# Attention: a third buffer of probabilities, and the copies of the raw output behind other exponentials

## The reference

```
x = x + attention(layernorm(x))   # 2 sequences of 512 tokens, 512 wide, 32 heads of 16
x = x + experts(layernorm(x))     # 8 experts of inner width 800, the best 2 of each token

q, k, v = proj(w_q), proj(w_k), proj(w_v)
scores = einsum('bhqd,bhkd->bhqk', q, k) / sqrt(16)
attn = softmax(scores, axis=-1)
out = einsum('bhqk,bhkd->bhqd', attn, v)
out = out.transpose(0, 2, 1, 3).reshape(B, S, HIDDEN)
return einsum('bse,oe->bso', out, w_o)
```

## Time and profile before

| what | value |
|---|---|
| median of 3 runs | 544.23 us (543.7 to 544.29) |
| the profiled execution, its own time | 544.15 us |
| its span in the trace | 542.4 us |
| PE, DVE, ACT busy over the span | 98%, 71%, 59% |
| the ordinary and whole steps of attention | from about 88 to 253 us |

### The profile page before, as it was taken

One profiled execution on the slowest core, in us unless ns is written; L12 is line 12 of the kernel. 1 busy time (PEld: TensorE's weight loads), 2 busy tenths in 40 slices (PEclk: granted clock), 3 DMA queues, 4 the chain that ended last, 5 costly groups with the idle time before them and its releaser, 6 DMA issues.

```text
span 542.4 us, 10567 instructions
## 1 busy us (share of the span) xinstructions
PE 529.6 (98%) x3925; PEld 390.7 (72%) x3925; DVE 385.8 (71%) x722; ACT 321.1 (59%) x476; POOL 117.3 (22%) x146
## 2 busy tenths in 40 slices
PE   8999999999999999999999999999999999999992
PEld 6887665344433334334878989999999999999991
DVE  7924767999998999943879986836648284666650
ACT  5322115888888878876372465746576575757540
POOL 4400111000120120722001320432342321242112
PEclk9999999999999999999989999999999999999998
DMA  8490367765775470022734797775846747586122
GB/s 304 142 112 6 48 107 91 99 89 90 95 98 72 89 143 14 24 91 100 280 119 171 234 379 250 204 255 111 320 72 219 224 155 267 129 296 159 39 36 38
DMA packets 29743, 78.24 MB, mean 144 GB/s; under 512 B 8572, under 2 KB 9596, under 8 KB 25210
## 3 DMA queue, kind: packets, MB, share of 16 engines
q1 hardware_dynamic: 24394, 68.84, 47.3%
q0 software_dynamic: 5296, 8.69, 8.7%
HBM read 53.11 MB, written 9.32 MB: 115 GB/s over the span
## 4 chain that ended last, share of the span: by engine, by line
PE 93%; DVE 2%; DMA 1%; issue 1%; POOL 1%; ACT 1%; POOLq 0%; DVEq 0%
PE ps L720 17%; PE ps L722 16%; PE ps L721 16%; PE ps_o L735 13%; PE ps L748 7%; PE ps L760 6%; PE ps_m L748 4%; PE ps L788 2%; PE ps_o L720 1%; PE ps_m L1017 1%; PE ps L1069 1%; PE ps L1072 1%; PE ps_o L721 1%; PE ps_o L722 1%; PE ps_m L720 1%
## 5 line engine op out<-in xcount | busy, mean ns | idle before, releaser
L1242 ACT ACTIVATE probs_t<-ps 128x1024 f32<-128x1024 f32 x128 | 125.5, 1023 | 27.6 <-PE ps_o L735 23.3
L1459 DVE TENSOR_REDUCE neg_max<-ps 128x1 fp32r<-128x512 f32 x171 | 111.1, 682 | 7.0 <-PE ps L748 4.5
L720 PE MATMUL ps<-xgT_hi,w_hi 128*128 128x256 f32 (+7 forms) x380 | 109.4, 288 | 0.0
L722 PE MATMUL ps<-xgT_hi,w_lo 128*128 128x256 f32 (+7 forms) x380 | 108.6, 286 | 0.0
L721 PE MATMUL ps<-xgT_lo,w_hi 128*128 128x256 f32 (+7 forms) x380 | 108.5, 285 | 0.0
L760 PE MATMUL ps<-q_stack,k_stack 49*128 49x512 f32 x256 | 83.1, 443 | 0.0
L735 PE MATMUL ps_o<-probs_t,v_ones 128*32 128x256 f32 (+1 forms) x944 | 79.6, 409 | 0.1
L720 PEld LDWEIGHTS ps<-xgT_hi,w_hi 128*128 128x128 f32 x380 | 72.0, 189 | 0.4 <-DVE xgT_lo L1734 0.2
L721 PEld LDWEIGHTS ps<-xgT_lo,w_hi 128*128 128x128 f32 x380 | 72.0, 190 | 0.1
L722 PEld LDWEIGHTS ps<-xgT_hi,w_lo 128*128 128x128 f32 x380 | 71.9, 189 | 0.0
L748 PE MATMUL ps<-k_stack,q_stack 48*128 48x512 f32 x171 | 68.4, 458 | 0.0
(11 more groups left out here) (326 smaller groups left out, 985.4 us busy)
## 6 DMA issues: line engine op xcount, KB each, us to landing
w_sb<-w SPq DMA_DIRECT2D x16, 1024.0 KB, 7.3
w_sb<-w SPq DMA_DIRECT2D x8, 1536.0 KB
w_sb<-w SPq DMA_DIRECT2D x8, 1152.0 KB, 8.1
q_stack<-q_hi SPq DMA_DIRECT2D x32, 128.0 KB, 4.9
k_stack<-k_hi SPq DMA_DIRECT2D x32, 128.0 KB, 4.6
q_stack<-q_lo SPq DMA_DIRECT2D x16, 128.0 KB, 4.4
k_stack<-k_lo SPq DMA_DIRECT2D x16, 128.0 KB, 5.7
q_hi<-o_raw SPq DMA_DIRECT2D x16, 128.0 KB, 4.8
```

What stands on the lines that cost most here:

```text
L720: pe.matmul(o, x_hi, w_hi, start=start, stop=False)
L722: return pe.matmul(o, x_lo, w_hi, start=False, stop=stop)
L1242: a.activation(probs_t[:, kc % 2, 2 * half:2 * half + 2, :], ps4[:, 2 * (n % 2):2 * (n % 2) + 2, :], ACT.Exp, scale=D ** -0.5).then_inc(s_ ...
L1459: v.tensor_reduce(neg_max[:, g % 2, col:col + 1], max_bank(g, u2), AX.X, ALU.max, negate=True).then_inc(s_mx, 1)
```

## The change

`probs_t` has three buffers in place of two, taken in turn over all chunks of all groups (m = 4 s + kc, buffer m % 3), so an exponential waits for the `pv` of three chunks before. The first half of `ps_o` was copied between exp(s,0) and exp(s,1), the second between exp(s,1) and exp(s,2); now the first is copied between exp(s,1) and exp(s,2), the second between exp(s,2) and exp(s,3). The whole copies stay between exp(s,1) and exp(s,2).

```diff
-        probs_t = sb(att, "probs_t", [P, 2, GH, S])
+        probs_t = sb(att, "probs_t", [P, 3, GH, S])
...
-                                     probs_t[:, kc % 2, j, q0:q1], start=(kc == q0 == 0),
+                                     probs_t[:, (g * TPB + kc) % 3, j, q0:q1], start=(kc == q0 == 0),
...
                 if p == 1 and s >= 1:
-                    raw_out(s - 1, 0 if b in whole else S // 2, S)
+                    raw_out(s - 1, 0, S if b in whole else S // 2)
...
-                        if m >= 2 and half == 0:
-                            a.wait_ge(s_pv, 2 * (m - 1))
-                        if p == 0 and half == 1 and s >= 1 and b + 1 not in whole:
-                            raw_out(s - 1, 0, S // 2)
+                        if m >= 3 and half == 0:
+                            a.wait_ge(s_pv, 2 * (m - 2))
+                        if p == half == 1 and s >= 1 and b not in whole:
+                            raw_out(s - 1, S // 2, S)
                         a.wait_ge(s_st, n + 1)
-                        a.activation(probs_t[:, kc % 2, 2 * half:2 * half + 2, :], ps4[:, 2 * (n % 2):2 * (n % 2) + 2, :],
+                        a.activation(probs_t[:, m % 3, 2 * half:2 * half + 2, :], ps4[:, 2 * (n % 2):2 * (n % 2) + 2, :],
                                      ACT.Exp, scale=D ** -0.5).then_inc(s_ex, 1)
```

## The result

The changed kernel takes 545.23 us (median of 11 runs, 544.82 to 546.04), the kernel before 543.99 us (median of 11, 543.51 to 545.24). The ratio is 1.0022, 95% interval 1.0014 to 1.0030: the change makes the kernel 0.2% slower, some 1.2 us. The forecast was 543.9 us and "no change", with a small gain (-0.3 us) as its sum, in a range of 542.6 to 545.7 us. The time lies inside the range, but the kernel moved the other way, by four times as much and clear of the noise.

The account below looks back on a forecast made before the run. The prediction took PE and DVE as full, ACT having slack. Its terms, -0.2 + 0.15 - 0.13 - 0.2 = -0.38 us, taken as -0.3, gave 543.85 us profiled, stated as 543.9 us, range 542.6 to 545.7.

Parts of the forecast that it names:

- ACT's waits for `pv`: ACT's 23.3 us of waits before exponentials: replaced by waits for `scores`, exp(s,0) running earlier being worth nothing by itself.
- The loss of 0.21 at pv(s-1,3,1): At an ordinary boundary, the first copy, now behind exp(s,1), makes pv(s-1,3,1) start 0.21 us after its natural start.
- exp(s,2) starts when its scores are there, X + 0.10: At an ordinary boundary, exp(s,2) starts at X + 0.10 us, which is also what ACT allows after the first copy.
- X: Natural start of pv(s-1,3,1) at an ordinary boundary: 1.24 us behind pv(s-1,3,0), 2.48 behind pv(s-1,2,1).
- releases pv(s,0,0) at X + 1.45 ... no further loss: Second copy ends at X + 1.40 and releases pv(s,0,0) at X + 1.45, PE's own time: no further loss, no cover.
- DVE is held up by at most 0.05 of it: At boundaries with DVE's shuffle, two `key_max` come 0.21 us later, but DVE is delayed by at most 0.05.
- The sum at a boundary without a shuffle: A boundary without DVE's shuffle costs 0.21 us in place of 0.24: -0.03 each, -0.2 us over 7.
- With a shuffle: At 5 boundaries with DVE's shuffle, PE comes out 0 to 0.05 us later; taken as +0.03 each, +0.15 us.
- The whole steps: At b = 29 and b = 57, PE's second pair of scores no longer waits: -0.13 and -0.2 us.
- The faster one: Rival: the buffer frees ACT and no new loss appears at the boundaries; 2.5 us gained, 541.7 us; chance 0.17.
- The slower one: Rival: copies come later than reckoned, pv(s-1,3,1) waits longer, loss 0.35; +1.3 us, 545.5 us; chance 0.23.
- its two signs: Signs of the slower rival: interval into pv(s-1,3,1) of 1.55 us or more, or pv(s,0,0) waiting for the second copy too.

## Why the prediction was wrong

- **ACT's waits for `pv` are worth nothing.** Right: the 23.3 us of them are gone, those for `scores` grew from 4.2 to 23.7 us, and the buffer alone left the boundary as it was.
- **The loss of 0.21 at pv(s-1,3,1).** Right, and term by term: exp(8,1) starts 1.35 behind pv(7,2,1) (reckoned 1.34), the copy 0.92 behind it (0.91), takes 0.38 (0.39), releases PE in 0.05 (0.05).
- **"exp(s,2) starts when its scores are there, X + 0.10".** Wrong by 0.06: it starts at X + 0.16 (173.43 - 173.27). The 0.78 came from the clean row of an exponential of an odd unit, which waits for one semaphore; exp(s,2) is of an even unit and waits for two, at 0.83 to 0.84.
- **"releases pv(s,0,0) at X + 1.45 ... no further loss".** This is the first of two steps that failed. It came at X + 1.57. I had given this release the 0.05 of an exponential, for an instruction that waits for one thing; it was 0.11. A row of the same kind stood in rows 7, the 0.14 behind the whole copy, and I used it for the wrong `pv`. I wrote that there was no cover and each 0.01 more is paid, and did not price it: 0.12 at this `pv` and 0.02 to 0.03 behind it. With one wait taken from each of the two instructions the seven boundaries without a shuffle gave the -0.2 us of the forecast.
- **"DVE is held up by at most 0.05 of it".** This is the second step that failed. With the first copy at its new place DVE's shuffle starts 0.1 us later in three groups and 0.2 us later in two, and PE comes out as much later: +0.8 us over the five boundaries in the change, where +0.15 was forecast. The two waits have no part in this, since it is still +0.7 us without them. The kernel without them was level with the one before (1.0001; its pv stretch is 0.22 us longer) and not 0.3 us faster. What in DVE's order makes it 0.1 in some groups and 0.2 in others no run takes apart.
- **The sum at a boundary without a shuffle.** Forecast -0.03, measured +0.10 to +0.15 at five of the seven. At the other two (to groups 3 and 5) it is 0: in the kernel before, their three intervals are 1.38, 1.41 and 1.30 and 1.37, 1.42 and 1.31, a loss of 0.37 and 0.38 that the forecast's 0.24 for each boundary left out. **With a shuffle**: forecast 0 to +0.05, measured +0.1 to +0.2.
- **The whole steps.** -0.13 and -0.2 forecast, -0.10 and -0.22 measured. The first is right by some luck: pv(7,0,0) came 0.12 earlier in its step than before and not 0.24, since this `pv` too waits for two semaphores (0.11 behind the copy, where I took 0.05) and the copy started 0.05 late, and the loss behind it was 0.06 smaller than reckoned (an interval of 1.53, reckoned 1.59).
- **The rivals.** The faster one is refuted. The slower one named 545.5 us and the place where a release of 0.14 might apply; its time was near, and one of its two signs came, pv(s,0,0) waiting for the second copy. But it put the longer release at pv(s-1,3,1), where it is 0.05, and not at pv(s,0,0). The chance for it, 0.23, was too low for a forecast whose second copy had a margin of 0.00.

## What to carry to other kernels

An engine with slack can still set the pace where two engines hand one bank to and fro: what counts there is the chain exponential, copy, product, not the busy share, and a wait that vanishes from a list of waits is worth only what somebody waited for behind it. Where a chain reckons out to a margin of zero, price each link by a row of the same kind, the number of semaphores waited for included, and take the unpriced remainder as a loss. More buffers can make a wait implied; then the wait itself can go, and in this kernel two such waits were worth 1 us. A delay ahead of a full engine need not be absorbed because that engine is late already, as DVE was here: look at what it does in the stretch behind, and price that apart.

## What the runs showed of the hardware

- An instruction that waited for two semaphores started later than one that waited for one: a load on PE 0.11 us after the copy that released it, against 0.04 to 0.05, and an exponential on ACT 0.84 against 0.78 to 0.79 behind the same `key_max` load. Taking one wait away moved each to the shorter time.
- PE's clock fell once in the kernel with the order alone. From 160 to 180 us the granted clock was 0.53 and 0.62, that is at its lower level of 1.2 GHz for most of the time, and the intervals there were 2.17 us where they are 1.24 at 2.4 GHz. It fell right behind the boundary to group 6, where PE was busy for 1.31 us of the 2.00 from 158 to 160 us. The same 1.73 and 2.12 us intervals stand at the five boundaries before it and the six behind it, at a granted clock of 1.00, so the stalls alone do not settle when it falls, and no run shows what does. The columns are the stretch, its length, busy time (and instructions) of PE, its loader, DVE, ACT and POOL, the granted clock, and the DMAs' share and rate:

```profile
150.00:160.00 10.00, 9.26 (x88) 3.32 (x86) 9.31 (x16) 7.02 (x9) 0.00 (x0) 1.00 0.71 95
160.00:170.00 10.00, 9.48 (x56) 3.05 (x56) 6.41 (x12) 5.07 (x7) 3.16 (x3) 0.53 0.70 93
170.00:180.00 10.00, 10.00 (x64) 3.03 (x60) 4.99 (x11) 5.97 (x8) 0.00 (x0) 0.62 0.10 29
```

- The runs of this kernel spread over 32 us (563 to 595), where those of all other kernels here spread over 1 to 2 us. The longer of its runs had the lower mean clock (0.98 in the one of 563.11 us, 0.91 in that of 595.03), so the spread goes with the time at the lower level; where the clock fell is known for the one run with a profile.
